# Packed 16-head attentions: products that nobody reads in the first steps, ScalarE's key builds first, and two bulk weight loads issued one block later

## The reference, cut to what matters

```python
# layer 0: a second pair of queries and keys, weighted by distance
scores = jnp.einsum('bhqd,bhkd->bhqk', q, k) * SCALE
esc = jnp.einsum('bhqd,bhkd->bhqk', eq, ek) * (1.0 / math.sqrt(HD)) * decay
attn = jax.nn.softmax(scores + ENT * esc, axis=-1)
# layer 2: a sparse mask that multiplies
scores = jnp.where(mask, raw, 0.0) / scale
attn = jax.nn.softmax(scores, axis=-1)
# mla: causal, with rotary columns
scores = jnp.where(causal[None, None], scores, jnp.finfo(scores.dtype).min)
```

## Time and profile before

| | |
|---|---|
| median of 3 runs | 795.06 us (794.1 to 798.94) |
| the profiled execution's own time | 795.14 us |
| its span | 793.3 us |
| TensorE matmul busy | 695.4 us (88%) |
| TensorE weight load busy | 558.9 us (70%) |
| VectorE busy | 413.9 us (52%) |
| GpSimd busy | 304.2 us (38%) |
| ScalarE busy | 248.4 us (31%) |
| mean granted TensorE clock | 0.939 of full speed |

### The profile page before, as it was taken

How to read it: one execution, slowest core, us unless ns; L and a number is a source line. 1 busy time by engine, 2 the same in 40 slices (tenths; PEclk the granted TensorE clock), 3 DMA queues, 4 the chain that set the end, 5 groups by cost and what they waited for, 6 DMA issues and landing times. The chain is left out here.

```text
span 793.3 us, 18728 instructions
## 1 busy us (share of the span) xinstructions
PE 695.4 (88%) x7083; PEld 558.9 (70%) x7083; DVE 413.9 (52%) x1108; ACT 248.4 (31%) x612; POOL 304.2 (38%) x351
## 2 busy tenths in 40 slices
PE   7997888899999889979997698788899868979997
PEld 5775777788888768854475586575435645879996
DVE  3756756554444265667634545646783566622211
ACT  1135301245455124135513301333463135111220
POOL 2337341456664121134225224701453375253111
PEclk9999996899999999899999789898999979889999
DMA  9503104778887419666424802200463162436603
GB/s 357 217 7 49 14 2 155 249 227 237 241 239 231 150 59 384 224 204 193 144 83 106 302 31 44 22 5 33 153 203 118 63 136 109 162 129 247 233 19 108
DMA packets 76558, 116.78 MB, mean 147 GB/s; under 512 B 44022, under 2 KB 57527, under 8 KB 73527
## 3 DMA queue, kind: packets, MB, share of 16 engines
q1 hardware_dynamic: 65141, 90.95, 35.7%
q0 software_dynamic: 6912, 17.31, 7.1%
q10 hardware_dynamic: 4418, 7.33, 2.5%
HBM read 100.42 MB, written 15.16 MB: 146 GB/s over the span
## 5 line engine op out<-in xcount | busy, mean ns | idle before, releaser
L285 PE MATMUL ps<-const_sb 128*128 128x128 f32 x898 | 120.1, 295 | 9.1 <-DMA const_sb<-in_consts 4.7
L285 PEld LDWEIGHTS ps<-const_sb 128*128 128x128 f32 x898 | 115.8, 209 | 12.5 <-issue 7.0
L1981 PE MATMUL ps<-l0e_xg_fm,l0e_ring 128*128 128x128 f32 x544 | 72.6, 277 | 6.5 <-ACT l0e_up_sb L2071 2.4
L1981 PEld LDWEIGHTS ps<-l0e_xg_fm,l0e_ring 128*128 128x128 f32 x544 | 67.5, 191 | 12.5 <-issue 8.4
L1058 PE MATMUL ps<-x_fm,w_sb 128*128 128x296 f32 x208 | 54.9, 415 | 4.7 <-PEq L242 4.4
L313 POOL TENSOR_TENSOR norm_r<-norm_ve,const_sb 128x2 f32<-128x2 f32 (+1 forms) x27 | 19.6, 725 | 93.6 <-DVE norm_ve L306 66.0
L2577 PE MATMUL ps<-l_w,const_sb 128*32 x132 | 48.8, 506 | 6.0 <-DMA l1e_own_gu<-in_l_experts 2.1
L1058 PEld LDWEIGHTS ps<-x_fm,w_sb 128*128 128x128 f32 x208 | 38.9, 190 | 18.2 <-issue 6.2
L1887 POOL DMA_INDIRECT l0e_y_scratch<-l0e_y_tm,l0e_rows_u x34 | 35.7, 1050 | 33.2 <-ACT l0e_y_tm L2095 29.3
L418 ACT ACTIVATE x_fm<-ps 128x256 f32<-128x256 f32 x35 | 12.6, 384 | 106.6 <-PE ps L394 106.5
L1872 POOL DMA_INDIRECT l0e_xg_tm<-x_scratch,l0e_rows_u x34 | 33.1, 974 | 22.6 <-PE ps L1945 11.4
(11 more groups left out here) (544 smaller groups left out, 1578.1 us busy)
## 6 DMA issues: line engine op xcount, KB each, us to landing
l0e_ring<-in_l_experts SPq DMA_DIRECT2D x34, 514.0 KB
l_w<-in_l_experts SPq DMA_DIRECT2D x1, 8704.0 KB, 27.0
expert_w<-in_l_experts SPq DMA_DIRECT2D x4, 2048.0 KB
l_more_w<-in_l_experts SPq DMA_DIRECT2D x4, 2048.0 KB
l1e_own_gu<-in_l_experts SPq DMA_DIRECT2D x11, 704.0 KB
l_w<-in_l_experts SPq DMA_DIRECT2D x1, 6144.0 KB, 18.5
l2e_own_gu<-in_l_experts SPq DMA_DIRECT2D x11, 512.0 KB
l0e_down_w<-in_l_experts SPq DMA_DIRECT2D x1, 4096.0 KB
```

The costliest lines, as they stand in the source:

```text
L285: pe.matmul(ps[:, bank, 0:P], ident, ident, start=True, stop=True)
L1981: mm = pe.matmul(ps[0:widths[m], which, m * P:(m + 1) * P], w_n[:, c:c + widths[m]], x_n[:, k, :], start=(k == 0), stop=(k == KT - 1))
```

## The change

Three things change in `attend`, which all three packed attentions use, and one in the blocks of layer 2.

- TensorE issues more products that nobody reads: `AHEAD[n]` ahead of the scores of step n (10, 16, 8 in layer 0; 10, 12, 8 in the two others; before: 8 at the start) and `BETWEEN[e]` ahead of the transposes of step e (4, 4, 0, 4). In front of the transposes the wait for the copied probabilities now comes before these products, and the wait for the exponential behind them.
- ScalarE makes keys of bunch 1 instead of the last bunch: in layer 0 the second keys of the bunches 1 and 2 (before 2 and 3), in the others the keys of bunch 1 (before 3). It makes them first, ahead of its copies of the queries to `q_left`.
- VectorE no longer makes one build of bunch 1 in layer 0.
- The loads of the weights of layer 3 and of the experts of layer 2 are both issued by SP in layer 2's output block.

```diff
-                ON_DVE = (4, 1, 0, 0) if second else (2, 0, 0, 0)
-                by_act = ((2, 1), (3, 1)) if second else ((3, 0),)
+                ON_DVE = (4, 0, 0, 0) if second else (2, 0, 0, 0)
+                by_act = ((1, 1), (2, 1)) if second else ((1, 0),)
+                AHEAD = (10, 16, 8, 0, 0) if second else (10, 12, 8, 0, 0)
+                BETWEEN = (4, 4, 0, 4)
...
                         act.preload_act_table(ACT.Exp)
+                        for n, m in by_act:
+                            act_keys(act, n, m)
                         for m, fm in enumerate(queries):
...
-                        for n, m in by_act:
-                            act_keys(act, n, m)
...
-                        stay_awake(pe, 8)
                         for n in range(STEPS + 2):
                             if n < STEPS:
+                                stay_awake(pe, AHEAD[n], 7)
...
                                 if e == 0:
                                     pe.wait_ge(s_pad, 1)
+                                if e >= 1:
+
+                                    pe.wait_ge(s_pfm, 2 * e)
+                                if e < len(BETWEEN):
+                                    stay_awake(pe, BETWEEN[e], 5)
                                 pe.wait_ge(s_probs, e + 1)
-                                if e >= 1:
-
-                                    pe.wait_ge(s_pfm, 2 * e)
...
+                    @block.sync
+                    def _(sp):
+                        if fetch is not None:
+                            fetch(sp)
...
-        def bring_l2(sp):
+        def bring_later(sp):
+            load(sp, "l3")
             sp.dma_start(l2_w[:, :, :], a["l2_experts"].rearrange("e p n -> p e n")).then_inc(s_l2w, 16)
...
-                    then=lambda sp: placed[4](sp, range(6)), layers=("l3",))
-            attend("l2a", placed, range(6, HEADS), ctx_fm, q_fm, k_fm, mask=const("sparse"), mask_op=ALU.mult, scale=0.25,
-                   then=bring_l2)
-            project_out("l2o", ctx_fm, "l2_o", row("l2_bo"), h, (xn, x0n, True, "w_ln1", latents_of(weight("mla_lat"))), to=xn)
+                    then=lambda sp: placed[4](sp, range(6)))
+            attend("l2a", placed, range(6, HEADS), ctx_fm, q_fm, k_fm, mask=const("sparse"), mask_op=ALU.mult, scale=0.25)
+            project_out("l2o", ctx_fm, "l2_o", row("l2_bo"), h, (xn, x0n, True, "w_ln1", latents_of(weight("mla_lat"))), to=xn,
+                        fetch=bring_later)
```

More of the change, by code:

```diff
@@ L923, in _ @@
                                     pe.wait_ge(s_pad, 1)
-                                pe.wait_ge(s_probs, e + 1)
                                 if e >= 1:
                                     pe.wait_ge(s_pfm, 2 * e)
+                                if e < len(BETWEEN):
+                                    stay_awake(pe, BETWEEN[e], 5)
+                                pe.wait_ge(s_probs, e + 1)
                                 for b in range(BLOCKS):
@@ L1186, in value_terms, with project_out @@
             return [(weight(w_name)[:, k, :], x_fm[:, k, :]) for k in range(KT)]
-        def project_out(tag, ctx_fm, w_name, bias, target, norm_args, affine=None, to=None):
+        def project_out(tag, ctx_fm, w_name, bias, target, norm_args, affine=None, to=None, fetch=None):
             two = affine is not None or to is not None
```

## The result

Measured side by side on one chip, eleven runs each, the changed kernel takes 792.97 us (median, 790.53 to 796.83) and the kernel before 797.64 us (792.5 to 805.43). The ratio is 0.9952, with a 95% interval of 0.9928 to 0.9975: a gain of 0.5%, or 3.8 us of 797.64. Every ratio here leaves out executions more than 1.5% above the fastest of the same kernel, so it can differ from the quotient of the two medians (here 4.7 us apart). The forecast was 6.0 us of 795.14. The direction was right and the time is in the range, but a third of the gain is missing.

A forecast was written before the change was run, and what follows sets the result against it. Key builds and softmax, with a slow clock, bound the attentions up to PV0, then TensorE; late instructions behind the bulk load delayed layer 2. Terms +0.7 - 0.4 - 7.1 + 0.5 + 0.3 = -6.0 from 795.14: 789.1 us, range 785.2 to 794.5.

The forecast's parts named there:

- Layer 2's attention, -7.1: Layer 2's attention without bulk loads: would look like mla's with the same products, 29.25 instead of 36.37 us.
- gaps of over 1 us in layer 2 without a load: Layer 2's attention: TensorE issue gaps this long after the load's removal would show the prediction wrong.
- first rival: Layer 2's attention: issue gaps stay since the load isn't their cause, 2.9 us, giving 792.0; chance 0.12.
- The products, +0.5 in mla and +0.7 in layer 0: Attentions of mla and layer 0: added unread products lengthen them, to 29.25 us in mla.
- The list for mla's head: Mla attention, block start to PV0: TensorE's products, scores and transposes add up to 12.1 us, against 11.20 before.
- third rival: The three attentions: products overrun, each TensorE-bound with 1.5 us more than summed, giving 793.6; chance 0.13.
- Layer 0's attention, +0.7: Layer 0's attention: +0.2 us from S0 to PV0 and +0.5 from products ahead of T3; bounds -0.5 and +2.0.
- Layer 2's projection, -0.4: Layer 2's projection block: ends about 0.4 us earlier without SP's issue of layer 3's load at its end.
- The loads in their new place, +0.3: Layer 2's output block and mla's value transfers: bulk loads there cost +0.3 us, bounds 0 and +3.
- The rival by which the gaps move along with the load: Layer 2's output and mla projection blocks: gaps move there and the clock falls, giving 795; chance 0.08.
- the rival of the other side: Attentions: the clock falls despite the products, 11.5 us more up to PV0 each; 800.6 or over 812; chance 0.04.

The follow-up runs named there:

- e5: The changed kernel with six unread products more before layer 0's attention and 15 in its output block (84 TensorE instructions): 775.07 us against 783.42, ratio 0.9908.
- e4: The changed kernel again, unaltered, in a single execution: 781.12 us against 783.14 for the kernel before.
- e10: The changed kernel again, unaltered, on another chip: 780.71 us against 781.43 for the kernel before, ratio 0.9983.
- e2: The changed kernel with the bulk loads back where they were before: 784.53 us, ratio 1.0038 to the kernel before.
- e6: The changed kernel with both bulk loads issued in the mla attention, behind its last value read: 783.51 us against 783.42, ratio 0.9989.
- e3: The changed kernel without the added products, eight at the start as before: 775.58 us, ratio 0.9914 to the kernel before.
- the fitted kernels: The changed kernel with products cut to the waits; two add 15 or 8 in layer 0's output block: ratios 0.9857, 0.9839, 0.9848 to the kernel before.
- e1: The kernel before with only both bulk loads moved to layer 2's output block: 777.15 us against 783.14, ratio 0.9935.

## Why the prediction was right or wrong, point by point

**Layer 2's attention, -7.1: the step that failed.** "Layer 2's attention should then look like mla's with the same products: 29.25 instead of 36.37 us" measured 31.68, 33.49 and 30.76, so -4.7, -2.9 and -5.6. The prediction's own sign of being wrong, "gaps of over 1 us in layer 2 without a load", came true with 1.3 and 1.1 us. The removal of the load did what it should: clock 1.00, no wait for `v_bd`, gaps of 4.2 us down to 3.4, the longest from 2.3 to 1.3. What I sized wrongly is what remains without a load. I took mla's gaps (1.3 us) as what such code has. But mla's are what *its position* has: e5 turned mla's 1.0 (0.8 and 1.0 in e4 and e10) into 3.8 by shifting the stream. Layer 2's went from 3.4 to 1.8, of which a part can be scatter (2.6 in e10). Of the 2.76 us between the two attentions of the changed kernel, 2.4 are issue gaps. The profile of before had the warning in layer 0's attention, 3.8 us of issue gaps without a bulk load (DMA share 0.19), the longest being

```profile
104.04 0.24 PE L947 MATMUL ps<-l0a_v_bd,l0a_p_fm 111*32 111x17 f32 x4 [1.66 <-issue]
```

and the prediction named layer 0 in its first rival but weighed mla's 0.6 alone. My first rival said that 2.9 us of gaps stay; that was nearly right in size, while its reason (the load is no cause) is refuted by e2 and e6. Both are causes: the stream gives the places, and the load makes one of them long. That the measured time, 792.97, lies so near this rival's 792.0 is partly luck, since 1.7 us of the miss stand in layer 0.

The Trainium skill, page "Runtime: NRT & Kernel Launch", section "Instruction fetch mechanics", states blocks of 16 KiB, 256 instructions, and that crossing one is mostly hidden. The distance agrees with the 128 matmuls and 128 weight loads between the gaps of e5, and with the packets: the page of the changed kernel has 60 instead of 58 for 424 instructions more. "Mostly hidden" fits the attentions badly: 105 of 224 transfers left a gap there, of up to 2.1 us without a bulk load and 3.54 with one. No row names the fetch as releaser, but its landing stands at a fixed distance, 1.23 to 1.58 us, ahead of the end of each gap. The prediction read the nature of the gaps rightly; what it had wrong is that without a load they shrink to mla's.

**The products, +0.5 in mla and +0.7 in layer 0.** The list for mla's head gave 12.1 us and it measured 12.54. The products were nearly right at 2.88 us from the first of 12 to the scores behind them (forecast 2.75), and the transposes were a little shorter than forecast, 0.66 and 0.75 instead of 0.84; a score step costs 0.66 us to the next instruction (504.88 to 505.54), not the 0.50 that I took from two score steps in a row. Behind PV0 the attention is 1.15 us shorter (17.53 to 16.38), not 0.4. So mla came to +0.2. The chain was right and its price too; but I never compared it with doing without. I had written that the products' head is TensorE's own list with nothing overtaking it. From there it was one step to ask how many products the waits could hold, and my third rival (overrun, 0.13) had only the hand-overs in mind. ScalarE's keys cut the wait that the 12 products were to fill from 1.66 us to 0.51 (e3), so most of them were pure length.

**What they cost overall.** e2 gives +3.0 us for the attention's part, e3 against the changed kernel 3 us for the products, and the fitted kernels, which have fewer of them in other places (and 15 or 8 more in layer 0's output block), are 1.4% below it on one chip. For e2 and e3 the intervals leave room for little or nothing, and I can't place their cost: by the blocks of the table, the changed kernel's five touched blocks sum to 132.95, 133.92 and 131.58 us, e3's to 132.15 and e1's to 133.67. The difference isn't in them. It would have to be in blocks whose code is untouched but stands up to 424 instructions further on in the stream, and layer 1's experts alone scatter by 4.6 us from profile to profile. It stays open.

**Layer 0's attention, +0.7.** Measured +2.4 in the first profile, against a before whose same code shows 37.47 and 39.29 us. With the mean of the two (38.38) and of the three of the changed kernel (39.41) it is +1.0. PV0 came 0.8 us later (15.59 to 16.36): from S0 to PV0 it is 12.60 us, where the list gave 12.0, again short by the score steps.

**Layer 2's projection, -0.4.** Not found in the changed kernel: 10.04, 10.52 and 10.50 against 9.91. In e1, whose TensorE instructions are those of before, it is there: 9.62. All of the difference is TensorE's wait at the block's end: without it the block takes 8.2 us in all twelve profiles. In the six with 10.03 us and more a 16 KB transfer of TensorE's instructions starts within this block, 8.9 to 10.4 us before its end; in the six with 9.91 and less none does. So the added products seem to have moved a crossing into the block. How a transfer so far ahead lengthens the wait isn't shown.

**The loads in their new place, +0.3.** The reasoning held and the cost is nothing: output block 18.02 us (forecast: still 18), mla projection 18.53 against 18.52. SP's issues in the changed kernel, answering to the earlier trace rows:

```profile
465.06 0.43 SPq L3278 DMA_DIRECT2D l_w<-in_l_experts  x1
485.19 2.31 SPq L1175 DMA_DIRECT2D v_scratch<-mlap_v_tm  x5
488.89 20.42 SPq L706 DMA_DIRECT2D mlaa_v_bd<-v_scratch  x32
```

The `v_scratch` writes start 20.1 us behind the issue of the experts' load, which lands after 20.3 us; the reads behind them take 20.42 us as before (20.43). The rival by which the gaps move along with the load is refuted (19.16 us from block to block, before 19.15).

**The sum.** With the first profile's terms: layer 0 +2.4, projection +0.1, layer 2's attention -4.7, loads 0, mla +0.2, that is -2.0; the two profiled executions differ by 1.7 us, the medians by 4.7 us, and the ratio says 3.8. The clock never fell in a way that made the change slower, so the rival of the other side (0.04) is out.

## What to carry to other kernels

Products that keep the clock up cost their full time wherever TensorE isn't waiting, so count them against the waits that are left *after* the other edits, in a profile that has those edits and no products: here 21 did as much for the clock as 38 in layer 2 and mla, with PV0 2.7 and 2.8 us sooner. Put bulk loads under stretches where TensorE goes through few instructions. And don't take a twin block as the measure of what a block will cost: the same code had 0.8 to 3.8 us of issue gaps without a load, by its place in the instruction stream and with some scatter at one and the same place. An issue gap can be checked: see whether a transfer of the instruction queue landed just before its end.

## What the runs showed of the hardware that was not expected

- In dense code of small matmuls, TensorE can stop every 256 instructions (128 matmuls with their weight loads). In the attentions 105 of 224 crossings left a gap, of up to 2.1 us without a bulk load, and of 3.54 and 3.22 us in e2 and e6 with one. In layer 0's left-over scores 256 instructions took 3.46 us, of which 2.26 were work.
- Each of these gaps ended 1.23 to 1.58 us after a 16 KB transfer of the instruction queue had landed. Under a bulk load that transfer took no longer (0.88 us) but started later, 1.20 and 0.97 us after TensorE had stopped.
- 84 instructions more ahead of it changed an attention of 29 us by 4.0 us (e5, mla).
- Behind waits at a block change of 2.31 and 3.15 us the clock was low for the first 20 matmuls (4.10 us instead of 2.47, e4 and e2), but behind one of 2.29 us it wasn't (e10).
- 15 unread products in a block whose TensorE waited 3.6 us went with a shorter block: 20.37 and 20.38 us, against 21.46 to 23.10 without them.
- The same untouched block, layer 0's experts, took 161 and 159 us on one chip and 149 to 152 on the others.
